# Shifted-window attention: heads in four row groups of three, both halves divided at once, 32-column value tiles

## What is computed

```
x  = x.transpose(0, 2, 3, 1); shortcut = x
xn = layernorm(x, norm1_g, norm1_b)                 # over the 96 channels
xs = roll(xn, (-4, -4), axis=(1, 2))
xw = windows of 8x8: 4 per image, 64 tokens each
qkv = xw @ qkv_w + qkv_b                            # 12 heads of 8
attn = softmax(q * 8**-0.5 @ k.T + bias + mask)     # 64x64 per head and window
out = (attn @ v) @ proj_w + proj_b
x  = shortcut + roll(out back)
x  = x + fc2(gelu(fc1(layernorm(x))))               # the MLP
```

## Time and profile before

| | |
|---|---|
| time, median of 3 runs | 540.69 us (535.23 to 543.65) |
| span of the profiled execution | 540.4 us |
| busy: PE / PEld / DVE / ACT / POOL | 96% / 63% / 68% / 56% / 33% |
| window attention, first to last `copy_k` | 15.4 to 238.7 us |

### The profile page before, as it was taken

One profiled execution on the slowest core, in us unless ns is written; L12 is line 12 of the kernel. 1 busy time (PEld: TensorE's weight loads), 2 busy tenths in 40 slices (PEclk: granted clock), 3 DMA queues, 4 the chain that ended last, 5 costly groups with the idle time before them and its releaser, 6 DMA issues. The chain is left out here.

```text
span 540.4 us, 23612 instructions
## 1 busy us (share of the span) xinstructions
PE 518.1 (96%) x9134; PEld 343.1 (63%) x9134; DVE 365.9 (68%) x1003; ACT 302.1 (56%) x763; POOL 178.3 (33%) x216
## 2 busy tenths in 40 slices
PE   7999999999999999998899999939999999999996
PEld 6777777777777777776674343339655655555553
DVE  1479999999999999997404354436556565656544
ACT  2278877777787778876435563103444444444432
POOL 8433444444434443344200220022433332333300
PEclk8599999999999999999999999957999999999999
DMA  4111111111111101100130132323454434444411
GB/s 83 29 42 32 30 30 46 29 30 30 30 29 24 26 24 29 29 3 2 45 75 21 46 93 71 88 49 79 121 146 124 115 101 118 121 114 105 117 51 32
DMA packets 41177, 32.51 MB, mean 60 GB/s; under 512 B 19240, under 2 KB 36776, under 8 KB 41128
## 3 DMA queue, kind: packets, MB, share of 16 engines
q1 hardware_dynamic: 37544, 26.11, 18.9%
q0 software_dynamic: 3584, 5.72, 4.8%
HBM read 18.36 MB, written 7.13 MB: 47 GB/s over the span
## 5 line engine op out<-in xcount | busy, mean ns | idle before, releaser
L383 POOL TENSOR_TENSOR scores<-scores,peak 128x768 f32<-128x768 f32 x64 | 94.3, 1473 | 135.3 <-DVE peak L552 135.3
L1224 POOL DMA_DIRECT2D x_stack<-padded_x x96 | 52.4, 548 | 97.4 <-PE ps_v L1497 63.4
L446 ACT COPY probs_t<-ps_probs 128x768 f32<-128x768 f32 x64 | 51.1, 799 | 40.7 <-PE ps_probs L706 40.7
L544 DVE TENSOR_TENSOR scores<-ps_scores,bias 128x768 f32<-128x768 f32 x64 | 61.3, 957 | 9.1 <-PE ps_scores L696 7.4
L552 DVE TENSOR_REDUCE peak<-scores 128x12 f32<-128x768 f32 x64 | 61.0, 953 | 2.4
L719 PE MATMUL ps_out<-v_blocks,probs_t 128*64 128x54 f32 x1536 | 57.2, 224 | 1.0 <-ACT out_t L451 0.9
L719 PEld LDWEIGHTS ps_out<-v_blocks,probs_t 128*64 128x64 f32 x1536 | 50.2, 138 | 12.3 <-issue 12.2
L706 PE MATMUL ps_probs<-ident,scores 128*128 128x128 f32 x384 | 55.0, 279 | 0.0
L440 ACT ACTIVATE scores<-scores 128x768 f32<-128x768 f32 x64 | 54.2, 846 | 0.6 <-POOL scores L383 0.6
L1037 ACT ACTIVATE hidden<-ps_hidden,fc_b_folded 128x512 f32<-128x512 f32 x48 | 29.1, 688 | 36.8 <-PE ps_hidden L978 36.8
L1497 PE MATMUL ps_qk<-x_stack,conv_w 40*32 40x256 f32 x1536 | 48.8, 379 | 0.0
(11 more groups left out here) (156 smaller groups left out, 900.2 us busy)
## 6 DMA issues: line engine op xcount, KB each, us to landing
x_stack<-padded_x SPq DMA_DIRECT2D x96, 54.0 KB
x_stack<-padded_x POOLq DMA_DIRECT2D x96, 54.0 KB, 2.7
padded_x<-x_pad SPq DMA_DIRECT2D x32, 121.5 KB, 2.5
x_sliced<-stream SPq DMA_DIRECT2D x48, 64.0 KB, 2.0
mixed<-y_sliced SPq DMA_DIRECT2D x48, 64.0 KB, 2.0
out<-y_sb SPq DMA_DIRECT2D x32, 96.0 KB, 2.0
x_now<-in_x SPq DMA_DIRECT2D x32, 72.0 KB, 1.8
stream<-in_x SPq DMA_DIRECT2D x32, 72.0 KB, 1.9
```

What stands on the lines that cost most here:

```text
L383: nc.gpsimd.tensor_tensor(sc, sc, peak[:, par, p, :].unsqueeze(2).to_broadcast((128, HEADS, WN)), ALU.subtract).then_inc(s["shifted"], 1)
L446: nc.scalar.copy(probs_t[:, :], ps_turned).then_inc(s["turned_copied"], 1)
L544: nc.vector.tensor_tensor(scores[:, par, p, :].rearrange("p (g c) -> p g c", g=NG), ps_scores[:, :, 0:GROUP * WN], bias[:, p, :].rearrange ...
L1224: engine.dma_start(x_stack[64 * half + i * HC:64 * half + (i + 1) * HC, slot, :, :], rows).then_inc(landed[slot], 16)
```

## The change

- Heads sit in four row groups of three instead of three of four. q and k are made with 128 weight columns (`WIDE`), where each group of 32 holds 24 channels of its own heads and 8 that the mask zeroes. `copy_k` writes 128x768. `score` has 8 matmuls (4 row groups, 2 windows) with 192 moved columns, into four banks.
- The values are put in the spare columns of score bank 2 and the projection in those of bank 3; `ps_b` is gone. So `score(t, 0)` now waits for `v_copied` of its own image and for `residual_done` of `t - 2` images, and `make_v` waits for nothing of the kind.
- `weigh` has 24 matmuls (6 head pairs, 4 tiles of 32 weight columns), 18 moved columns each; `make_v` has 16, of 32 weight and 48 moved columns. The two halves write side by side in `ps_out`.
- `weigh_heads(t)` divides both halves at once, one reciprocal of 128x24 and one product of 128x192; `turn_heads(t)` and `copy_ot(t, par)` do both halves in one place too.
- The order in `step` changes. PE: q and k, `weigh(t,1)`, `make_v(t+2)`, `project(t-1)`, `turn(t+1,0)`, `score(t+2,0)`, `turn_heads(t)`, `turn_back(t+3)`, `weigh(t+1,0)`, `score(t+2,1)`, `turn_tokens(t+4)`, `turn(t+1,1)`. ACT: `copy_v(t+2)` moves ahead of `inverse_deviation`, `scale` and `copy_turned(t+1,0)`. DVE: one `weigh_heads(t)` behind `copy_k(t+2)`, none between `find_peak(t+2,0)` and `add_bias(t+2,1)`.
- At the start the qkv bias comes as one row of 288 floats instead of three columns, and the head mask as two loads; `fold_q_k_v` adds the row through matmuls of one weight row, 22 matmuls in place of 3. `w_qkv` is written by two copies.

The diff, without the hunks that only change shapes, counts and names:

```diff
     normed = sb("normed", [C, N])
-    q_sb = sb("q_sb", [C, N])
-    k_blocks = sb("k_blocks", [C, GROUP, N])
-
-    v_blocks = sb("v_blocks", [128, 2, PAIRS, 2, HP + 2, 2, VC])
+    q_sb = sb("q_sb", [WIDE, N])
+    k_blocks = sb("k_blocks", [WIDE, TRIO, N])
+
+    v_blocks = sb("v_blocks", [128, 2, PAIRS, 2, HP, 2, VC])
     scores = sb("scores", [128, 2, PAIRS, SC])
...
     ps_a = bank("ps_a")
-    ps_b = bank("ps_b")
     ps_tokens = ps_a[:, 0, 0:2 * C].rearrange("p (h c) -> p h c", c=C)
...
     ps_folded = ps_scores[0:C, 2, 0:3 * C]
-    ps_q, ps_k = (ps_scores[0:C, g, GROUP * WN:GROUP * WN + N] for g in range(2))
-    ps_v = ps_b[:, 0, 0:2 * C].rearrange("p (w q d) -> p w q d", w=2 * PAIRS, d=HD)
-    ps_proj = ps_b[0:C, 0, 0:N]
+    ps_q, ps_k = (ps_scores[:, g, N:2 * N] for g in range(2))
+    ps_v = ps_scores[:, 2, TRIO * WN:TRIO * WN + 2 * C].rearrange("p (w q d) -> p w q d", w=2 * PAIRS, d=HD)
+    ps_proj = ps_scores[0:C, 3, N:2 * N]
     ps_turned = ps_probs.rearrange("p b c -> p (b c)")[:, 0:SC]
-    ps_pv = ps_out[:, 0, 0:HEADS * VC].rearrange("p (h c) -> p h c", c=VC)
-    ps_ot = ps_out[0:C, 0, 384:512]
+    ps_pv = ps_out[:, 0, 0:PAIRS * HEADS * VC].rearrange("p (a h c) -> p a h c", h=HEADS, c=VC)
+    ps_ot = ps_out[0:C, 0, N:2 * N].rearrange("p (a n) -> p a n", a=PAIRS)
+    ps_biases = ps_out[:, 0, 0:3]
+    ps_b_proj = ps_out[0:C, 0, 3:4]
     first_homes = [ps_scores[:, 0, :], ps_scores[:, 1, :], ps_scores[:, 2, :], ps_a[:, 0, :]]
...
                  (cols[:, 0:1], column("L0_conv_norm1_g")), (cols[:, 1:2], column("L0_conv_norm1_b")),
-                 *((cols[:, 2 + k:3 + k], a["L0_conv_qkv_b"][k * C:(k + 1) * C].rearrange("(c a) -> c a", a=1))
-                   for k in range(3)),
-                 (head_mask[:, :], a["c_head_mask"]))
+                 (b_row[:, :], a["L0_conv_qkv_b"].rearrange("(a c) -> a c", a=1)),
+                 (head_mask[0:C, :], a["c_head_mask"][:, 0:TRIO]), (head_mask[C:WIDE, :], a["c_head_mask"][0:32, 0:TRIO]))
         second = (*((shift_mask[WN * top:WN * (top + 1), left, :], a["c_shift_mask"][WN * left:WN * (left + 1), top])
...
-        def copy_ot(t, p, par):
-            act.wait_ge(s["ot_ready"], t * 2 + p + 1)
+        def copy_ot(t, par):
+            act.wait_ge(s["ot_ready"], t + 1)
             need(act, s["proj_ready"], t - 1)
-            nc.scalar.copy(shifted(out_t[:, par, :], p), window_rows(ps_ot, p)).then_inc(s["ot_copied"], 1)
+            for p in range(PAIRS):
+                nc.scalar.copy(shifted(out_t[:, par, :], p), window_rows(ps_ot[:, p, :], p)).then_inc(s["ot_copied"], 1)
...
         def step(t, half, par):
-            if real(t):
-                copy_ot(t, 0, par)
             if is_image(t, B - 1):
...
                 copy_q(t + 2)
+                copy_v(t + 2, par)
             if real(t + 3):
...
             if real(t):
-                copy_ot(t, 1, par)
+                copy_ot(t, par)
             if real(t + 1):
...
                 copy_normed(t + 3)
-            if real(t + 2):
-                copy_v(t + 2, par)
             if is_image(t, B - 2):
...
             need(dve, s["scores_ready"], t * 2)
-            nc.vector.scalar_tensor_tensor(out=k_blocks[:, :, :], in0=ps_k.unsqueeze(1).to_broadcast((C, GROUP, N)),
+            nc.vector.scalar_tensor_tensor(out=k_blocks[:, :, :], in0=ps_k.unsqueeze(1).to_broadcast((WIDE, TRIO, N)),
                                            scalar=b_k[:, 0:1],
-                                           in1=head_mask[:, :].unsqueeze(2).to_broadcast((C, GROUP, N)),
+                                           in1=head_mask[:, :].unsqueeze(2).to_broadcast((WIDE, TRIO, N)),
                                            op0=ALU.add, op1=ALU.mult).then_inc(s["k_copied"], 1)
...
-        def weigh_heads(t, p):
-            u = t * 2 + p
-            dve.wait_ge(s["pv_ready"], u + 1)
-            need(dve, s["heads_ready"], u)
-            nc.vector.reciprocal(recip[:, :], ps_pv[:, :, HD]).then_inc(s["recip_ready"], 1)
-            dve.wait_ge(s["recip_ready"], u + 1)
-            need(dve, s["ot_ready"], u)
-            nc.vector.tensor_tensor(heads_out[:, :].rearrange("p (h d) -> p h d", d=HD), ps_pv[:, :, 0:HD],
-                                    recip[:, :].unsqueeze(2).to_broadcast((128, HEADS, HD)), ALU.mult).then_inc(s["heads_ready"], 1)
+        def weigh_heads(t):
+            dve.wait_ge(s["pv_ready"], (t + 1) * 2)
+            need(dve, s["heads_ready"], t)
+            nc.vector.reciprocal(recip[:, :, :], ps_pv[:, :, :, HD]).then_inc(s["recip_ready"], 1)
+            dve.wait_ge(s["recip_ready"], t + 1)
+            need(dve, s["ot_ready"], t)
+            nc.vector.tensor_tensor(heads_out[:, :, :].rearrange("p a (h d) -> p (a h) d", d=HD),
+                                    ps_pv[:, :, :, 0:HD].rearrange("p a h d -> p (a h) d"),
+                                    recip[:, :, :].rearrange("p a h -> p (a h)").unsqueeze(2).to_broadcast((128, PAIRS * HEADS, HD)),
+                                    ALU.mult).then_inc(s["heads_ready"], 1)
...
             if real(t):
-                weigh_heads(t, 1)
+                weigh_heads(t)
             if is_image(t, B - 2):
...
                 find_peak(t + 2, 0, par)
-            if real(t + 1):
-                weigh_heads(t + 1, 0)
             if is_image(t, B - 2):
...
             pe.wait_ge(consts_in, 16 * FIRST)
+            pe.wait_ge(one_set, 1)
             for k in range(3):
-                nc.tensor.matmul(ps_out[0:C, 0, k:k + 1], w_in[:, k * C:(k + 1) * C], cols[:, 1:2],
-                                 start=True, stop=True, skip_group_check=True).then_inc(pe_set, 1)
+                for g in range(NG if k < 2 else SLICES):
+                    at = k * C + g * (GROUP_C if k < 2 else 32)
+                    home = ps_biases[32 * g:32 * g + 32, k:k + 1]
+                    nc.tensor.matmul(home, w_in[:, at:at + 32], cols[:, 1:2], start=True, stop=False, skip_group_check=True)
+                    mm = nc.tensor.matmul(home, b_row[:, at:at + 32], one[:, :], start=False, stop=True, skip_group_check=True)
+                mm.then_inc(pe_set, 1)
...
         def make_v(t):
-            need(pe, s["residual_done"], t - 2)
-            heads = w_qkv[:, 2 * C:3 * C].rearrange("c (q e d) -> c q e d", e=2, d=HD)
+            heads = w_qkv[:, 2 * WIDE:2 * WIDE + C].rearrange("c (q e d) -> c q e d", e=2, d=HD)
             for window in range(2 * PAIRS):
-                for e in range(2):
-                    mm = nc.tensor.matmul(ps_v[64 * e:64 * e + 64, window, :, :], normed[:, window * WN:(window + 1) * WN],
+                for part in range(PARTS_W):
+                    e, at = part // 2, window * WN + part % 2 * 32
+                    mm = nc.tensor.matmul(ps_v[32 * part:32 * part + 32, window, :, :], normed[:, at:at + 32],
                                           heads[:, :, e, :], start=True, stop=True, skip_group_check=True)
...
             need(pe, s["biased"], u)
+            if p == 0:
+                pe.wait_ge(s["v_copied"], (t + 1) * 2)
+                need(pe, s["residual_done"], t - 2)
             for g in range(NG):
...
                     q, k = q_sb[ch, tokens], k_blocks[ch, :, tokens]
-                    mm = nc.tensor.matmul(ps_scores[64 * w:64 * w + 64, g, 0:GROUP * WN], q, k, start=True, stop=True,
+                    mm = nc.tensor.matmul(ps_scores[64 * w:64 * w + 64, g, 0:TRIO * WN], q, k, start=True, stop=True,
                                           skip_group_check=True)
...
             if is_image(u, 0):
-                pe.wait_ge(set_up, 6)
-            pe.wait_ge(s["v_copied"], (t + 1) * 2)
-            need(pe, s["ot_copied"], u)
+                pe.wait_ge(set_up, 5)
+            if p == 0:
+                need(pe, s["ot_copied"], t * PAIRS)
             pe.wait_ge(s["turned_copied"], u + 1)
             for q in range(HP):
-                for top in range(2):
-                    mm = nc.tensor.matmul(ps_out[64 * top:64 * top + 64, 0, q * 2 * VC:(q + 3) * 2 * VC],
-                                          probs_t[:, q * 128 + 64 * top:q * 128 + 64 * top + 64],
-                                          v_blocks[:, par, p, top, q:q + 3, :, :].rearrange("p q e c -> p (q e c)"),
+                for part in range(PARTS_W):
+                    at = q * 128 + 32 * part
+                    mm = nc.tensor.matmul(ps_pv[32 * part:32 * part + 32, p, 2 * q:2 * q + 2, :],
+                                          probs_t[:, at:at + 32], v_blocks[:, par, p, part // 2, q, :, :],
                                           start=True, stop=True, skip_group_check=True)
...
-        def turn_heads(t, p):
-            u = t * 2 + p
-            pe.wait_ge(s["heads_ready"], u + 1)
-            nc.tensor.transpose(ps_ot, heads_out[:, :], ident[:, :]).then_inc(s["ot_ready"], 1)
+        def turn_heads(t):
+            pe.wait_ge(s["heads_ready"], t + 1)
```

(23 more changed lines are left out.)

58 lines of the change are left out of this document (35 added, 23 removed).

## The result

The changed kernel takes 554.74 us, median of 6 runs (553.18 to 556.72), against 538.28 for the kernel before on the same chips (6 runs, 535.23 to 543.65). The ratio is 1.033, 95% interval 1.027 to 1.039: slower by 16 us, where the forecast had 7 more. Ratios compare fast executions alone, those within 1.5% of the fastest of the same kernel.

A forecast was written before the change was run, and what follows sets the result against it. DVE's own sum was taken as the bound (7.01 us a period). Period 7.01 - 0.66 + 0.67 + 0.16 = 7.18, taken as +5.1 over 30 periods; 540.4 + 5.1 + 3.6 (start) - 1 (end) = 548.1, forecast 548 us, range 534 to 560.

The forecast's parts named there:

- same: Whole kernel: time within 2% (11 us) of no change, between 530 and 551.5 us; chance 0.58.
- What bounds the kernel before: Steady window attention: DVE never waits, its own sum sets the 7.01 us period; PE's slack is about 0.1 us.
- What leaves DVE: DVE's list per image: smaller `copy_k` and one `weigh_heads` fewer save 0.66 us.
- DVE's share: DVE's busy share in the steady stretch falls from 96% to some 88%.
- What the new wait costs: First score waits for the residual, so DVE stands ahead of `add_bias(0)`: about 0.67 us an image (0.61 to 0.75).
- ACT's second wait: `weigh(t+1,0)` waits for ACT's copies of the turned heads, delaying `add_bias(1)` by 0.16 us an image (0 to 0.3).
- PE's blocks: PE's steady blocks: `weigh` 0.58 us, `make_v` 0.56, score 0.56; all ahead of the residual.
- first and third rivals: First: tiles don't gain, `weigh` keeps 0.88, 563 us, chance 0.16. Third: record pairs run one after another, 614, chance 0.03.
- the second: Rival: DVE does not stand ahead of the score, period 6.35 plus little, 524 us; chance 0.09.
- The start: `fold_q_k_v`, 22 matmuls at 0.23 us each, 5.1 in all; net +3.6 us with a load saved (-0.6 to +6.1).
- The end: Last three steps of the pipeline: a shorter chain and shorter `weigh` save 1 us (0 to 2).
- the bubble: DVE's idle stretch between the residual and `add_bias(0)`, about 0.67 us an image (0.61 to 0.75).

The follow-up runs named there:

- c2: Kernel before with only the 32-column tiles of `weigh` and `make_v` (18 moved columns in `weigh`): 528.44 us, ratio 0.987.
- a1: Changed kernel, but `add_residual` reads an SBUF constant instead of the projection, so the first score need not wait for it: 554.06 us, ratio 1.037.
- c1: Kernel before with the tiles and both halves divided, turned and copied at once, old banks and three row groups kept: 529.32 us, ratio 0.981.
- b3: Changed kernel, but from the third image on the score leaves out its fourth row group (6 tiles instead of 8): 552.06 us, one run.
- s3: Changed kernel with the start's fold matmuls grouped by shape within q, k and v, six blocks, all sums kept: 549.90 us, ratio 1.027.
- b1: Changed kernel with the fold's 11 `w_in` matmuls first, then the 11 with the bias row; q and k biases lose part: 550.13 us, ratio 1.020.

## Where the forecast was right, and where it got half the size

The time lies in the range of 534 to 560, and slower it is; but the largest chance, 0.58, was on "same", and the 0.33 for slower was too low. The span was to grow by 7.7 and grew by 14.6: 5.7 more in the periods, 1.1 less at the start, 2.3 more at the end.

**What bounds the kernel before**: wrong. DVE did wait for PE, at both `add_bias`, too shortly to be marked; c2 shows it, with 0.17 us an image gained by a change to PE alone.

**What leaves DVE**: right. `copy_k` 0.90 start to start (0.94 foreseen), reciprocal 0.30, product 0.36, the one division 0.63 (0.67). Start to start 0.74 leaves DVE's list, 0.66 foreseen. **DVE's share**: 85% for 88%.

**What the new wait costs**: this is the step that failed. The mechanism (residual, hop, whole score, DVE) is in the rows as told, but DVE stands longer (residual to `add_bias` 1.40 for 0.53, so 0.87, not 0.67), and the forecast took this stand for the main cost. a1 says otherwise: without the residual's wait the stand is 0.64, as small as forecast, and the period is 7.37 all the same. The stand lies beside the path that sets the period. Two terms of it were too small. From score to DVE I took 0.76 from the earlier trace rows, the last score of the pipeline; in the steady stretch it is 0.84 or 0.85: 120.96 to 121.81 in the earlier trace rows, 129.86 to 130.70 and 132.01 to 132.85 in c1. I had passed over the first because DVE wasn't marked as waiting there. 0.84, less the 0.11 for columns, plus 0.04 for two more tiles as b3 prices them, is the 0.77 measured. And the hop from DVE to PE, which no row of before showed, is 0.15, not 0.06.

**ACT's second wait**: named rightly, and this is the path that sets the period, 5.04 to `add_bias(1)` for 4.82. The 0.22 are what the period of 7.18 lacks to 7.40. More than half of it, 0.12, is again the price from score to DVE (0.77 for 0.65), 0.05 lies between `weigh` and score (0.56 for 0.51), the rest in smaller steps. Measured as the forecast did, from start to start, DVE is late by 0.25 for 0.16; the 0.17 in the bracket counts from the end of the record. The stations are each within 0.25: `copy_turned` 2.54 after `copy_k` (2.39), copies 3.22 (3.08 for ACT, 3.18 for the heads), `weigh` 3.71 (3.66), score 4.27 (4.17), `add_bias(1)` 5.04 (4.82). Sum of this image: 7.01 - 0.74 + 0.87 + 0.25 = 7.39, measured 7.40. What I didn't see is that the two paths to `copy_ot` are nearly equal (3.08 and 3.18 in my own sum, with the heads last; measured, ACT is last, 3.22 to 3.10), so that the first wait costs nothing that the second wouldn't: a1. That 0.66 saved and 0.67 lost cancelled in my sum was luck in part, as the 0.67 wasn't what cost the time.

**PE's blocks**: right. `weigh` 0.57 to 0.61 (0.58), `make_v` 0.53 (0.56), score 0.58 (0.56). The first and third rivals fall with these rows, and the second with the 0.91.

**The start**: 0.194 a matmul for 0.23; the fold 4.26 for 5.1. In s3 the changes of shape are what costs, as the forecast argued. The rule of the Trainium skill, "TensorEngine Tiling (Array Packing)", section "Key Properties", that a new tiling mode drains the engine, agrees: at the full level a matmul takes 0.15 when the shape changes with each, and four of one shape take 0.17. The price is these runs': 0.14 a change at the full level. **The end**: wrong in sign, +1.3 for -1, and open. The rest behind the last `copy_k` lies between 299 and 310 us over the fourteen profiled kernels, which all share the MLP and the channel attention, so 2 us there can't be put down to an edit.

**The chances**: the range held the time, but more lay above 551.5 than I gave (0.33). The bounds of the bubble (0.61 to 0.75) left out what the steady rows showed.

Open: whether the trio layout would gain with the waits gone, and what the new order costs by itself. No run keeps the fences off while DVE and ACT still read values and projection from the score banks. Four banks for scores, two for the turned scores, `ps_a` and `ps_out` are the eight that the kernel before used too; other places for values and projection within them weren't tried.

## What to carry to other kernels

Saving work on the busiest engine pays only while its input is made ahead of it, and an engine whose records touch one another may still be waiting: look for a distance from its producer that stays the same in every image. A tile that moves into another's bank takes over its fence, the wait until everyone is out of the bank: list who must leave the bank, and where that stands in the order, before counting what the edit saves. Read a producer's length where the pipeline is steady, also from rows where nobody waits, and before removing one wait look for a second path of nearly equal length that ends in the same place. Matmuls of different tile shapes are best issued in blocks, not in turn.

## Behaviour of the hardware that was not expected

Matmuls of 32 columns in four column groups follow each other very closely: 48 records of `weigh` take 0.57 to 0.61, some 12 ns each. When the shape changes every two records, two of them cost 0.15 at the full level of the clock and 0.19 at the half level, where a block of eight records takes 0.17 at the full one.

Executions of one kernel differ by about 8 us, and the profiles put that down to a stretch at the half level of TensorE's clock (1.2 GHz), mostly at the start. The kernel before ran 26 times at 531.9 to 538.0 us and 15 times at 539.7 to 545.2 us in the runs of this study, with a mean granted clock, where it is recorded, of 0.972 to 0.984 and of 0.959 to 0.971; in its profile (540.4) the granted clock is 0.50 from 10 to 25 us. b1 had one execution of 542.10 and three near 550; in the profiled one, that of 542.10, the 20 fills behind q and k take 1.94, in the changed kernel 3.52:

```profile
12.60 1.94 PE L113 MATMUL ps_probs<-blank 96*96 96x96 f32 x20
```

```profile
19.16 3.52 PE L113 MATMUL ps_probs<-blank 96*96 96x96 f32 x20
```

The stretch can lie elsewhere: c1's profile (533.4, while two executions took 525) has the full level by 15 us, but half of it behind the last `copy_k`, at the start of the MLP:

```profile
240.00:245.00 5.00, 5.00 (x27) 3.25 (x26) 4.55 (x33) 2.21 (x5) 0.00 (x0) 0.50 0.01 3
```

All executions of the changed kernel lie in 553 to 557, the five without the profile with a mean of 0.961 to 0.966, and the profiled one has the long fills. So a part of the 16 us between the medians may be that the kernel before mostly starts at the high level and this one did not; between two profiles with long fills (3.41 in the kernel before) it is 14.6, and against the three slower executions of the kernel before (540.7 to 543.7) it is 12. Why a start falls at one level or the other isn't shown. The changed kernel's granted clock, in the page's 40 slices, reads full from the first on, although its fills ran at the length of the half level:

```profile
PEclk9999999999999999999999999976999999999999
```
